# Gated cross-attention kernel: late duos, tail and combines placed anew, and the order of steps 4 and 5 changed

## The reference, cut to what matters

```python
def step(carry, xs):                      # one of 128 time steps, all 32 batches
    r = decay * r + kt * vt               # k = v = ctx, so ctx squared
    retained = (qt * r).reshape(B, D)     # q = layernorm(x)
    inp = retained @ Wi.T + bi
    gate = sigmoid(inp @ Wg.T + bg)
    blended = gate * state + (1.0 - gate) * inp
    state = tanh(blended @ A.T + inp @ Bm.T)
    out = state @ Wo.T + bo
x = x + tanh(g_xattn) * outs
fx = layernorm(x)
shared_out = swiglu(fx @ w_shared_in) @ w_shared_out
probs = softmax(fx @ w_gate + gate_bias); top 2 of 8 experts
hid = swiglu(fx @ w1_shared)
routed = sum over the two chosen e of probs[e] * (hid @ w2[e])
x = x + tanh(g_ffn) * (shared_out + routed)
```

## Time and profile before

| | us |
|---|---|
| runs of the kernel before | 481.08, 480.12, 478.55 (median 480.12) |
| profiled execution: its time | 479.74 |
| its span, first to last instruction | 478.0 |
| PE busy | 424.7 (89%) |
| DVE busy | 359.7 (75%) |
| ACT busy | 224.3 (47%) |
| POOL busy | 194.4 (41%) |
| mean granted TensorE clock | 0.974 |

### The profile page before, as it was taken

How to read it: one execution, slowest core, us unless ns; L and a number is a source line. 1 busy time by engine, 2 the same in 40 slices (tenths; PEclk the granted TensorE clock), 3 DMA queues, 4 the chain that set the end, 5 groups by cost and what they waited for, 6 DMA issues and landing times.

```text
span 478.0 us, 12307 instructions
## 1 busy us (share of the span) xinstructions
PE 424.7 (89%) x4348; PEld 355.9 (74%) x4348; DVE 359.7 (75%) x1305; ACT 224.3 (47%) x526; POOL 194.4 (41%) x231
## 2 busy tenths in 40 slices
PE   5987699998988989999989889998997979999890
PEld 4974588787877878988778779887986856865650
DVE  2687979898998777758897777779776675566785
ACT  3564456676746354636464546363643331331300
POOL 3011302442437530202275665432676551447641
PEclk9999889999999999999999999999998988999996
DMA  6786050505243453753441179793236675599862
GB/s 158 203 242 159 2 154 3 143 22 136 45 135 87 147 113 82 162 112 99 102 112 57 45 138 226 169 168 122 100 111 131 169 144 130 166 216 219 207 239 105
DMA packets 110283, 63.08 MB, mean 132 GB/s; under 512 B 80400, under 2 KB 100240, under 8 KB 110224
## 3 DMA queue, kind: packets, MB, share of 16 engines
q1 hardware_dynamic: 105104, 48.66, 42.2%
q0 software_dynamic: 5120, 13.64, 10.4%
HBM read 24.26 MB, written 27.53 MB: 108 GB/s over the span
## 4 chain that ended last, share of the span: by engine, by line
PE 51%; DVE 26%; issue 8%; ACT 3%; DMA 3%; POOL 3%; DVEq 0%; POOLq 0%; ACTq 0%
PE bank L577 11%; PE bank L588 10%; PE bank L635 10%; PE rec L719 5%; PE rec L602 4%; DVE u_hi L1315 4%; DVE r L1424 2%; PE rec L607 2%; DVE u_full L1317 2%; PE bank L867 2%; PE rec L577 2%; ACT state L1004 2%; DVE hs L1650 1%; DVE ret L1437 1%; PE rec L588 1%
## 5 line engine op out<-in xcount | busy, mean ns | idle before, releaser
L1004 ACT ACTIVATE state<-rec 128x64 f32<-128x64 f32 x128 | 36.6, 286 | 156.3 <-PE rec L607 156.2
L1315 DVE SCALAR_TENSOR_TENSOR u_hi<-gt,state 128x64 f16<-128x64 f32 x127 | 39.2, 309 | 68.7 <-ACT state L1004 68.5
L1897 POOL DMA_INDIRECT hrows<-hid_rows,slots_i x52 | 58.5, 1124 | 72.9 <-ACT state L1004 34.4
L1910 POOL DMA_INDIRECT yg<-yrows,slots_i x52 | 53.6, 1032 | 40.4 <-ACT state L1004 18.4
L602 PE MATMUL rec<-u_hi,a_hi 128*128 128x32 f16 x512 | 48.3, 196 | 15.8 <-DVE u_hi L1315 15.7
L602 PEld LDWEIGHTS rec<-u_hi,a_hi 128*128 128x128 f16 x512 | 37.0, 99 | 23.9 <-DVE u_hi L1315 20.3
L602 PE MATMUL rec<-u_hi,a_lo 128*128 128x32 f16 x512 | 47.7, 194 | 0.0
L1840 POOL TENSOR_TENSOR hs_lo<-hs,hs_hi 128x512 f16<-128x512 f32 x14 | 16.2, 1157 | 56.0 <-ACT hs_hi L1205 56.0
L607 PE MATMUL rec<-u_lo,a_hi 128*128 128x32 f16 x512 | 36.5, 195 | 1.0
L602 PEld LDWEIGHTS rec<-u_hi,a_lo 128*128 128x128 f16 x512 | 35.5, 99 | 1.9 <-issue 0.9
L1317 DVE SCALAR_TENSOR_TENSOR u_full<-gt,state 128x64 f32<-128x64 f32 x127 | 35.8, 282 | 0.0
(11 more groups left out here) (299 smaller groups left out, 1390.9 us busy)
## 6 DMA issues: line engine op xcount, KB each, us to landing
yrows<-squares_w SPq DMA_DIRECT2D x20, 256.0 KB
yrows<-squares_sh SPq DMA_DIRECT2D x18, 256.0 KB, 3.0
x_sb<-in_x_dram SPq DMA_DIRECT2D x16, 256.0 KB, 3.4
c_sb<-in_ctx_dram SPq DMA_DIRECT2D x64, 64.0 KB
xr_sb<-in_x_dram SPq DMA_DIRECT2D x16, 256.0 KB, 3.9
hrows<-zeros SPq DMA_DIRECT2D x4, 1024.0 KB, 5.9
raw_w<-in_L_ffn_w_dram SPq DMA_DIRECT2D x8, 256.0 KB, 5.0
out_dram<-raw_w SPq DMA_DIRECT2D x8, 256.0 KB, 2.5
```

The source lines that it names most:

```text
L1004: act.activation(step_of(state[i % 2], t), step_of(rec[i % 2], t), ACT.Tanh, scale=1.0 / PSCALE).then_inc(st_ready, 1)
L1315: dve.scalar_tensor_tensor(out=u_hi[p][:, :, :], in0=gate, scalar=1.0, in1=old, op0=ALU.add, op1=ALU.mult).then_inc(uh_ready, 1)
L1897: pool.indirect_dma_start(hrows[q % 2], bass.IndirectOffsetOnAxis(ap=slots_i[q][:, at:at + 1], axis=0), hid_rows[t % 6][:, s, :, :].rearra ...
L1910: pool.indirect_dma_start(yg[t % FETCHED][:, s, pick, :], None, yrows[q % 2][0:blocks_of(q) * P, :], bass.IndirectOffsetOnAxis(ap=slots_i[ ...
```

## The change

PE: in slot 4 `addend_bm` goes away; in slot 5 it comes first, then the duo, then the second transposition with the counting products. ACT: the second layer norm moves from between tanh 4 and tanh 5 to behind tanh 5; so the gate's tanh follows the first layer norm directly, and duo copies go in front of `xn_hi`. DVE: `context_turned` moves from slot 4 to slot 6. In iteration 15 duo 27 moves from slot 5 to slot 4. The pairs of tile 13 and their adds move one place later. Combines, four gathers of tile 5 and four of tile 6 get new places. For tile 15 the tanh of the routing comes ahead of `hid_hi`, and the shared sum behind the routing weights.

```diff
-              + [(15, slot) for slot in (0, 1, 2, 3, 5)] + ...
+              + [(15, slot) for slot in range(5)] + ...
-        COMBINE = {(11, 6): (0,), (12, 6): (1, 2), (15, 2): (3,), (15, 6): (4,), (16, 3): (5,), (16, 5): (6,), (17, 1): (7,), (17, 2): (8,),
-                   (17, 4): (9,), (17, 5): (10,), (17, 7): (11, 12)}
+        COMBINE = {(11, 6): (0,), (12, 6): (1, 2), (15, 5): (3,), (15, 6): (4,), (16, 3): (5,), (16, 5): (6,), (16, 7): (7,), (17, 1): (8,),
+                   (17, 2): (9,), (17, 3): (10,), (17, 7): (11, 12)}
@@ PE, iteration
                 recurrence(i, 4, k)
                 gate_product(a, k)
-                addend_bm(a, k)
                 duos_at(i, 4)
...
-                if d == TILES - 3:
-                    pe.wait_ge(y_ready, evacuated(TILES - 1, 2))
-                    pair(0, d)
...
                 recurrence(i, 5, k)
+                addend_bm(a, k)
+                duos_at(i, 5)
                 x1_transposed(c, k)
                 for q in range(len(CHUNKS)):
                     if d == last_of(q):
                         prefix(q)
-                duos_at(i, 5)
                 if d == TILES - 3:
+                    pe.wait_ge(y_ready, evacuated(TILES - 1, 2))
+                    pair(0, d)
                     pair(1, d)
-                    pair(2, d)
... (slot 6: pairs 2 and 3 in place of 3 and 4; slot 7: pair 4)
@@ ACT, iteration
                 x_normalised(f, k)
+                gate_tanh(a, k)
+
+                tanh_step(i, 5, k)
                 x1_normalised(c, k)
-                gate_tanh(a, k)
-
-                tanh_step(i, 5, k)
+                y_evacuated_at(i, 5)
                 if k.has(c):
                     ... xn2_hi copy
-                y_evacuated_at(i, 5)
 
                 tanh_step(i, 6, k)
+                if 2 <= i <= 4:
+                    w2_high(3 * (i - 2) + 1)
                 context_squares(f, k)
                 y_evacuated_at(i, 6)
@@ DVE, iteration
                 gated_state(i, 4, k)
                 combined_at(i, 4)
+                if d < TILES - 1:
+                    shared_sum(d, k)
...
-                context_turned(f, k)
...
                     weighed(d, k)
+                if d == TILES - 1:
+                    shared_sum(d, k)
...
                 gated_state(i, 6, k)
+                context_turned(f, k)
@@ POOL
-            spread(GATHERS, range(3, 7), ... + [(15, 0)] + [(16, t) for t in (0, 1, 2, 3, 4, 4, 4, 4)])
+            spread(GATHERS, range(3, 7), ... + [(15, 0)] + [(16, t) for t in (0, 0, 1, 1, 2, 2, 3, 3)])
```

More of the change, by code:

```diff
@@ L396, in gated_layer @@
               + [(12, slot) for slot in (0, 1, 2, 3, 5)] + [(13, slot) for slot in (0, 1, 2, 5)] + [(14, 5)]
-              + [(15, slot) for slot in (0, 1, 2, 3, 5)] + [(16, slot) for slot in (0, 1, 1, 2, 2, 3, 4, 5)]
+              + [(15, slot) for slot in range(5)] + [(16, slot) for slot in (0, 1, 1, 2, 2, 3, 4, 5)]
               + [(17, slot) for slot in (0, 0, 1, 1, 2, 2)])
@@ L828, in duos_at @@
                         pe.wait_ge(inp_ready, TILES)
-                    elif i == TILES - 1 and slot == 5:
+                    elif i == TILES - 1 and slot == 4:
                         pe.wait_ge(y_ready, evacuated(i, 1))
@@ L983, in iteration @@
                     last.then_inc(lg_done, 1)
+                if d == TILES - 3:
+                    pe.wait_ge(pair_used[0], k.nth(d))
+                    pair(4, d)
                 if d == TILES - 2:
@@ L1097, in x1_normalised, with log_tanh @@
                 last.then_inc(xn2_ready, 1)
+            def log_tanh(d, k):
+                if not k.has(d):
+                    return
+                act.wait_ge(ld_ready, k.n(d))
+                if k.has(d - 1):
+                    act.wait_ge(numden, k.n(d - 1))
+                act.activation(flat(lt[:, :, :]), flat(ld[:, :, :]), ACT.Tanh, scale=0.5).then_inc(lt_ready, 1)
             def w2_high(e):
@@ L1230, in iteration @@
                         act.copy(hid_rows[d % 6][:, :, 0, :], hid[:, :, :]).then_inc(hid_hi, 1)
[L1231 to L1234, removed]
+                if d < TILES - 1:
+                    log_tanh(d, k)
                 y_evacuated_at(i, 3)
@@ L1355, in combine_second, with shared_sum @@
                 last.then_inc(combined, 1)
+            def shared_sum(d, k):
+                if not k.has(d):
+                    return
+                if d < 8:
+                    dve.wait_ge(setup_pe, 8)
+                else:
+                    dve.wait_ge(w2_lo, d - 7)
+                dve.wait_ge(so_done, k.n(d))
+                dve.scalar_tensor_tensor(out=flat(acc[d][:, :, :]), in0=bank[B_SO][:, :], scalar=out_un[:, 0:1],
+                                         in1=flat(x1[d % 2][:, :, :]), op0=ALU.mult, op1=ALU.add).then_inc(acc_ready, 1)
             def combined_at(i, slot):
@@ L1667, in iteration @@
                 if e == TILES - 3:
+                    add_pair(4, e, k)
                     add_pair(5, e, k)
@@ L1929, in _ @@
             spread(SCATTERS, range(7, 11), [(13, t) for t in (0, 1, 2, 3, 4, 4, 5, 5, 6, 6, 7, 7)] + slots(14)[:4])
-            spread(GATHERS, range(3, 7), [(14, t) for t in (4, 5, 5, 6, 6, 7, 7)] + [(15, 0)] + [(16, t) for t in (0, 1, 2, 3, 4, 4, 4, 4)])
+            spread(GATHERS, range(3, 7), [(14, t) for t in (4, 5, 5, 6, 6, 7, 7)] + [(15, 0)] + [(16, t) for t in (0, 0, 1, 1, 2, 2, 3, 3)])
             spread(SCATTERS, range(11, 13), slots(15))
```

39 lines of the change are left out of this document (15 added, 24 removed).

## The result

The changed kernel takes 472.21 us (median of 4 runs, 471.36 to 473.69) against 479.6 for the kernel before (4 runs beside it). The ratio is 0.9845, with an interval of 0.9803 to 0.9886, so the change gains 1.6%. The prediction said 475.9, range 471.5 to 481.5, and faster with 0.64. Direction and range held. The measured gain of 7.4 us was nearly twice the forecast of 3.9, so some steps must be wrong.

What follows compares the result with a forecast made beforehand. PE, busy 89% of the span, bounds the kernel: its list plus stalls. Terms -2.6 + 0 + 1.2 + 1.1 + 0.9 - 3.0 - 1.5 = -3.9 from 479.74 give 475.8, stated as 475.9; range 471.5 to 481.5.

Steps and rivals of the forecast that it cites:

- tiles 5, 6, 9, 10: Plain tiles: transposition stays in place, step 6 follows directly behind it; gain 0.64 each, 2.6 in all.
- tiles 2 to 4: L1747, held by POOL's low half of expert weights, keeps step 6 in place; gain 0, at most 0.5 each.
- duo tiles 7, 8, 11, 12, 13: Tiles with a duo in slot 5, and tile 13: late u_lo and a later transposition; cost 1.2 together.
- context in slot 6: L1417 moves into DVE's slot 6: no cost in plain tiles, 0.7 in tile 12, 0.4 elsewhere; cost 1.1.
- tile 14: Transposition and counting products come behind duo 22; idle grows from 2.9 to about 4 us; cost 0.9.
- tile 15: Duo 27 fills the wait for hid_lo; step 6 4.9 earlier, less pair 4 and 0.6 for the clock; gain 3.0.
- tail: The 1.44 us wait in front of duo 35 goes because its copy comes ahead of xn_hi; gain 1.5.
- the second stall: Plain tiles, in front of step 6: PE's 0.48 us idle, hanging on the gate's tanh.
- A: Rival: both stalls of the four plain tiles go, tile 15 runs at full clock; about 470, chance 0.12.
- B: Rival: idle times in tiles 14 and 15 end in half clock, a read takes 6.5 us; 479, chance 0.22.
- C: Rival: context in slot 6 chains DVE, ACT's squares and tanh 7, up to 0.7 a tile; 484, chance 0.08.
- D: Rival: step 5 waits for u_lo in every tile as in tile 7; 482, chance 0.06.

Runs made afterwards that it cites:

- The scatter experiment: The changed kernel with GpSimd issuing the scatter or gather of slot 3 behind rs2, nr2 and the low part of hid: 478.18 us, ratio 0.9974.
- the steady half: The kernel before with only the new order of slots 4 and 5 and context in slot 6; first run, lacking ScalarE's w2_high line: 478.68 us, ratio 0.9992.
- the late half: The changed kernel with the order of slots 4 and 5, the context and w2_high as before: 476.05 us, ratio 0.9941.
- the second run of the steady half: The kernel before with the steady half, now also with w2_high ahead of the context's squares in tiles 2 to 4: 474.68 us, ratio 0.9903.

## Why the prediction was right, and where its sum was wrong

Each step of the sum against the pair of profiled executions (478.0 and 470.4), with the context's share taken from the run that put it back:

| step | forecast | measured |
|---|---|---|
| tiles 5, 6, 9, 10 | -2.6 | -2.8 |
| tiles 2 to 4 | 0 | +0.1 |
| duo tiles 7, 8, 11, 12, 13 | +1.2 | +0.8 |
| context in slot 6 | +1.1 | -0.5 |
| tile 14 | +0.9 | -0.1 |
| tile 15 | -3.0 | -3.5 |
| tail | -1.5 | -0.2 |
| start, tile 1 | 0 | -1.6 |
| a read in tile 11 | 0 | +0.3 |

The measured column adds up to -7.5, the forecast to -3.9. The rows for tile 14, the tail, tile 1 and the read come from one execution of each kernel and hold its luck. (In tile 15, 4.83 were gained and pair 4, 1.3 us, now stands behind step 7: 3.5. The same 1.3 is taken off the rest: 72.94 against 71.88 + 1.3.)

**Right, mechanism and size: the plain tiles.** The reading that POOL's shift fixes the transposition and only the second stall goes gave 0.64 a tile. With the context in its old place, tiles 5, 6, 9 and 10 gain 0.77, 0.70, 0.65 and 0.67. The scatter experiment shows the first half of the sentence: when `nr2` came earlier, and only then, the transposition did too. Tiles 2 to 4, forecast at 0 because L1747 is held behind POOL's second low part, gained nothing: step 6 is at +5.46, +5.47 and +5.72 in both kernels. The row shown for tile 3 was no chance: the instruction takes 1.13 to 1.14 us in all three tiles, in the kernel before and, as L1762, in the changed one. For L1324 the hold is shown by the run that moved L1857: 0.27 without it, 1.23 to 1.26 under it. The Trainium skill ("SBUF — State Buffer", section "Who interferes with whom") says that a VectorE instruction with two inputs in SBUF contends with a GpSimd instruction that reads SBUF, and that one with a single SBUF input doesn't, outside the modes that use both ports. The traces agree: L1324 reads `gt` and `state` and is held; L1375, whose first input is a PSUM bank, took 0.75 while L1857 ran beside it. L1375 had begun first, so the second half is not put to a strict test.

**Right: duo tiles and tile 15.** Steps 6 of tiles 7, 8, 11, 12 and 13 were forecast (the old place plus the step's cost) at +6.0, 5.84, 5.95, 6.49 and 5.0 and came at 6.02, 5.84, 6.05, 6.48 and 4.84. The cause, the low part on `u_hi` of step 5, is shown by the run that moved it. What the prediction left out is that in tiles 8 and 12 the context's move by itself gains the same wait for the one-hot rows, 0.43 each; beside the new order nothing of it is seen. Tile 15 came out within 0.1 at step 6; seven further executions with the same order in it have 7.59 to 7.85. Only the 0.6 set aside for the lower clock was not needed.

**Wrong: "Context turned in slot 6 ... Cost 1.1".** The step counted what the instruction displaces in its new slot (0.7 in tile 12: measured 0.58) and nothing for the slot that it leaves. In slot 4 it stood in front of the one-hot rows, and these in front of `u_hi` 6, `u_lo` 6 and `cn`: 1.33 us in four tiles. In the sentence "in plain tiles ... no cost" the sign of the term was lost. The rest of the 0.4 for tiles 4, 7, 8 and 11 did not show either (below 0.05, but for the read in 11).

**Mis-sized by the execution: tile 14 and tile 1.** For tile 14 the forecast's 0.9 is not refuted by the -0.1, and that the total came out lower here is luck. Six kernels with the new order there took 24.28 to 26.73 (mean 25.2), three with the old 22.94 to 25.17 (mean 24.2): 1.0 between the means, inside a scatter that the read's landing makes. As forecast, PE was ready for the duo sooner, at r4 + 4.13 where it had been + 4.97. The idle time did not grow to 4 us only because the read was there sooner by as much: from the last scatter's issue to the duo 7.1 us passed, in the kernel before 8.0. Tile 1 was not in the forecast. Both kernels stand there 3.0 us without work at the same place; 1.6 us and more behind it the clock was 0.50 in one and 1.00 in the other:
```profile
60.80:64.20 3.40, 3.40 (x19) 3.31 (x18) 2.40 (x10) 2.15 (x5) 1.02 (x2) 0.50 0.33 89
```
```profile
61.60:64.20 2.60, 2.56 (x31) 2.44 (x32) 2.23 (x7) 1.75 (x5) 0.19 (x1) 1.00 0.33 101
```
(the kernel before, then the changed one). Twelve executions with the new order took 21.68 to 22.99 in tile 1, mean 22.6; the two with the old took 23.13 and 24.71. In the thirteen executions other than the changed kernel's a spell at the lower level begins in this wait (2.5 to 3.0 us) or within 2 us of its end, whatever the order. So 21.68 was a lucky one; of the 1.45 about 0.5 is left between 23.13 and the mean, and whether that is real stays open.

**Wrong: "Tail ... Gain 1.5".** The wait at the copy did go: it is absent in the steady half and in the changed kernel, and back at 1.44 in the late half. What the step lacked is the reads, which stand behind it as the next thing to wait for. In the changed kernel one was issued at 410.11:
```profile
410.11 1.23 SPq L487 DMA_TRANSPOSE raw_sh<-hrows  x1
```
```profile
416.48 0.28 PE L635 MATMUL bank<-w_hi,raw_sh 128*128 x1 [0.91 <-DMA raw_sh<-hrows]
418.97 0.28 PE L635 MATMUL bank<-w_hi,raw_w 128*128 x1 [0.36 <-issue]
...
447.39 0.28 PE L635 MATMUL bank<-w_hi,raw_sh 128*128 x1 [1.71 <-DMA raw_sh<-hrows]
```
Two waits are new and the last grew from 1.23 to 1.71. Whether the late tiles, 5 us sooner, made the reads late is not shown. With the late tiles as before the rest took 70.35 in the second run of the steady half, 1.5 less than before as forecast, but 72.47 in the first, which has the same code there: its last read was waited for 3.28 us and not 1.99, and the clock was 0.50 behind it. A term of 1.5 can't be told from one execution where the same code differs by 2.1.

**The rivals.** A (all stalls go, 470) had the time nearly right and the mechanism wrong: the first stall of the plain tiles is still there (0.77). Of B the lower clock in tile 14 came, 1 us into the duo; that in tile 15 and the read of 6.5 us did not (the longest took 5.2). C's chain does exist and costs 4.0 us, but only without the one line that the change moved with it; the prediction weighed C without seeing that `w2_high` decides it. D did not come. (By the weights that it names, nine tenths of 0.64 and a quarter of 0.22, "faster" is 0.63 and not 0.64.)

## What to carry over

Price a moved instruction twice: what it delays where it arrives, and what it sets free where it was; the second had the larger number here. When two engines hold each other up, look for a move in the idle engine's queue: one wait of GpSimd was worth 2.0 us here. But look first for the transfer that hangs on the last instruction of that queue. And compare executions stage by stage before explaining a total: plain tiles repeated to 0.04 us, while one tile with a late read, and the tail, moved by 2 with the same code.
